# One subtraction of the last SwiGLU chunk on another engine, and two ScalarE functions in the other order

## The reference

```
norm(x, t; g, b) = (t Wg^T + g) * x / sqrt(mean(x^2) + 1e-6) + (t Wb^T + b)
y   = x + attention(norm1(x, cond))            # 16 heads of 16 channels, softmax over 64 keys
z   = y + (silu(n Wgate^T) * (n Whid^T)) Wout^T   with n = norm2(y, cond), 1024 hidden channels
out = x + z
```

## Time and profile before

| | |
|---|---|
| time, median of 3 runs | 1078.95 us (1076.1 to 1081.28) |
| profiled execution | 1077.67 us, span 1075.9 us, mean TensorE clock 0.992 |
| TensorE busy | 1032.2 us, 96% |
| VectorE busy | 673.7 us, 63% |
| ScalarE busy | 423.5 us, 39% |
| GpSimd busy | 339.5 us, 32% |
| DMA | 21.67 MB, 20 GB/s over the span |

### The profile page before, as it was taken

One profiled execution on the slowest core, in us unless ns is written; L12 is line 12 of the kernel. 1 busy time (PEld: TensorE's weight loads), 2 busy tenths in 40 slices (PEclk: granted clock), 3 DMA queues, 4 the chain that ended last, 5 costly groups with the idle time before them and its releaser, 6 DMA issues.

```text
span 1075.9 us, 22083 instructions
## 1 busy us (share of the span) xinstructions
PE 1032.2 (96%) x8240; PEld 919.7 (85%) x8240; DVE 673.7 (63%) x1306; ACT 423.5 (39%) x903; POOL 339.5 (32%) x284
## 2 busy tenths in 40 slices
PE   6879999999999999999999999999999999999987
PEld 5768889889888988988888888988988898898876
DVE  4645766566666656766666676657666665666543
ACT  3433343444334343343434434344433434334232
POOL 4313233232333223233232323323233323324142
PEclk9979999999999999999999999999999999999999
DMA  4100000010100001010010100001010000100000
GB/s 169 41 1 21 2 24 18 1 39 0 39 0 19 19 0 39 0 39 0 0 39 0 39 0 25 14 0 39 0 39 0 19 19 0 39 0 21 1 21 19
DMA packets 18968, 21.67 MB, mean 20 GB/s; under 512 B 640, under 2 KB 18240, under 8 KB 18816
## 3 DMA queue, kind: packets, MB, share of 16 engines
q1 hardware_dynamic: 18720, 21.24, 5.9%
q10 hardware_dynamic: 224, 0.10, 0.0%
HBM read 12.95 MB, written 8.39 MB: 20 GB/s over the span
## 4 chain that ended last, share of the span: by engine, by line
PE 67%; issue 23%; POOL 5%; ACT 2%; DVE 2%; DMA 0%; POOLq 0%; ACTq 0%; DVEq 0%; SPq 0%
PE ps L824 8%; PE ps L737 6%; PE ps L809 6%; PE ps L739 6%; PE ps L738 5%; PE ps L817 5%; PE ps L832 4%; PE ps L842 4%; PE ps L845 4%; PE ps L835 4%; PE ps L843 4%; PE ps L833 4%; POOL h_lo L247 4%; PE ps L744 1%; PE ps L853 1%
## 5 line engine op out<-in xcount | busy, mean ns | idle before, releaser
L247 POOL TENSOR_TENSOR h_lo<-shared,h_hi 128x512 fp32r<-128x512 f32 x128 | 164.7, 1286 | 360.5 <-ACT h_hi L371 313.3
L577 DVE SCALAR_TENSOR_TENSOR shared<-shared,ps 128x512 f32<-128x512 f32 x128 | 87.8, 686 | 128.1 <-ACT shared L366 127.6
L737 PE MATMUL ps<-out_w_hi,h_hi 128*128 128x256 f32 x512 | 154.1, 301 | 9.5 <-POOL h_lo L247 9.5
L366 ACT ACTIVATE shared<-ps 128x512 f32<-128x512 f32 x128 | 76.4, 597 | 194.1 <-PE ps L835 125.2
L739 PE MATMUL ps<-out_w_hi,h_lo 128*128 128x256 f32 x512 | 144.4, 282 | 0.0
L738 PE MATMUL ps<-out_w_lo,h_hi 128*128 128x256 f32 x512 | 143.7, 281 | 0.0
L824 PEld LDWEIGHTS ps<-values,probsT 128*128 128x128 f32 x1024 | 129.8, 192 | 13.2 <-ACT probsT L376 8.0
L376 ACT ACTIVATE probsT<-ps 128x512 f32<-128x512 f32 x128 | 74.7, 597 | 163.8 <-PE ps L817 163.8
L824 PE MATMUL ps<-values,probsT 128*128 128x66 f32 x1024 | 130.8, 271 | 4.0 <-ACT probsT L376 4.0
L371 ACT CAST h_hi<-shared 128x512 fp32r<-128x512 f32 x128 | 78.9, 616 | 99.7 <-DVE shared L584 99.7
L563 DVE TENSOR_REDUCE row_max<-ps 128x8 f32<-128x512 f32 x128 | 87.8, 686 | 37.7 <-PE ps L809 36.7
(11 more groups left out here) (101 smaller groups left out, 2150.9 us busy)
## 6 DMA issues: line engine op xcount, KB each, us to landing
x_in<-in_x SPq DMA_DIRECT2D x16, 512.0 KB, 3.4
out<-result SPq DMA_DIRECT2D x15, 512.0 KB, 2.9
shared<-in_attT SPq DMA_DIRECT2D x1, 1024.0 KB, 7.0
shared<-in_gateT SPq DMA_DIRECT2D x1, 1024.0 KB, 8.9
shared<-in_hidT SPq DMA_DIRECT2D x1, 1024.0 KB, 4.8
shared<-in_outT SPq DMA_DIRECT2D x1, 1024.0 KB, 5.5
out<-result SPq DMA_DIRECT2D x2, 256.0 KB, 2.2
result<-in_modT SPq DMA_DIRECT2D x1, 256.0 KB, 4.7
```

Source lines behind the costliest of these rows:

```text
L247: nc.gpsimd.tensor_tensor(h_lo[:, j % 2, :], h[:, :], h_hi[:, j % 2, :].bitcast(F32), ALU.subtract).then_inc(h_lo_done, 1)
L737: nc.tensor.matmul(dst, a_hi, b_hi, start=first, stop=False, skip_group_check=skip)
```

## The change

The low half of chunk 7 (the last of a tile) is formed by VectorE between its h of that chunk and the gains of the second normalisation, in place of GpSimd. It waits for the cast of chunk 7, for the low half of chunk 6 (still from GpSimd, so that the shared counter stays in order), and for the down product that used the same buffer. In ScalarE's list the exponential of pair 0 stands ahead of the tanh of chunk 0.

```diff
@@ GpSimd, iteration
                     inverse_rms(t, ms2, ms2_done, mse2, mse2_done, inv2, inv2_done, scaled2)
-                if mlp:
-                    low_hidden(t - 1, 7)
                 if attend:
                     low_norm2(t, 0)
@@ ScalarE, iteration
                 if alone(t):
                     keep_input(t)
+                if attend:
+                    exp(t, 0)
                 if mlp:
                     tanh(t - 1, 0)
                 if attend:
-                    exp(t, 0)
                     exp(t, 1)
@@ VectorE
+            def last_low_hidden(u):
+                j = CHUNKS - 1
+                dve.wait_ge(h_hi_done, CHUNKS * u + j + 1)
+                dve.wait_ge(h_lo_done, CHUNKS * u + j)
+                wait(dve, down_mm, CHUNKS * u + j - 1)
+                nc.vector.tensor_tensor(h_lo[:, j % 2, :], h[:, :], h_hi[:, j % 2, :].bitcast(F32),
+                                        ALU.subtract).then_inc(h_lo_done, 1)
@@ VectorE, iteration
                 if mlp:
                     act_and_gate(t - 1, 7)
+                    last_low_hidden(t - 1)
                 if attend:
                     for c in range(CH):
                         gain(t, c, 2, PAIR + 2 + c, xT2_done, xn2, xn2_lo_done, gained2)
```

## The result

The changed kernel takes 1072.90 us (median of 18 runs, 1066.94 to 1074.84), the kernel before 1079.53 (18 runs, 1076.06 to 1081.46): a ratio of 0.9931, 95% interval 0.9917 to 0.9946. The profiled execution took 1071.17 us, span 1069.4.

A forecast was written before the change was run, and what follows sets the result against it. TensorE's work (busy 96% of the span) plus its standstills bounds the kernel. Seams 8.0 + last tile 0.57 - seam behind iteration 15 0.44 - exchange 0.6 = 7.5 us less, so 1070.8 us, range 1067.5 to 1075.

The forecast's parts named there:

- down product earlier, 14 seams: Tile seams behind iterations 1 to 14: TensorE's last down product starts 0.57 us earlier each, 8.0 us in all.
- gains later: VectorE's gains and shifts of the next normalisation, queued behind the new subtraction, start 0.08 to 0.23 us late.
- scores and low passes wait: TensorE behind the seam: neither score products nor first chunk's low passes wait; 0.7 us of cover left at the latter.
- tanh late by the exchange: ScalarE behind the seam: tanh of chunk 0 starts 0.04 us late, costing 0.6 us over 15 iterations.
- new wait of the gate product: TensorE's gate product of chunk 1 would wait 0.3 to 0.5 us for h of chunk 0, 15 times.
- distance of the iterations: Time from one tile seam to the next falls from 63.83 to 63.30 us; forecast wrong if unchanged or below 63.1.
- seam behind iteration 15: Seam without scores or attention, low passes already waiting for GpSimd's xn_lo: later gains cost 0.44 us (0.3 to 0.55).
- end of the last tile: Nothing covers the subtraction there, so moving it to VectorE saves 0.57 us (0.5 to 0.63).
- The forecast's base: Starting time for the 7.5 us gain, set between the profiled 1077.67 us and the three-run median 1.3 higher.
- Rival A: Gate product of chunk 1 held only by TensorE's queue, so the exchange gains 4 us or more: 1066 or lower; chance 0.05.
- Rival B: TensorE's seam gain spent waiting at scores or low passes, half of 8 us or more gone: 1074 to 1078; chance 0.10.
- Rival C: Late exp 0 holds tanh, h of chunk 0 and gate product; slower from 0.54 us delay, 1078.6 or 1090; chance 0.05.

The follow-up runs named there:

- e1: Changed kernel without its exchange (tanh of chunk 0 again ahead of exp 0), only the low half of chunk 7 on VectorE: 1072.31 us, ratio to before 0.9928.
- e2: Kernel before with only the exchange (exp 0 ahead of tanh 0), low half of chunk 7 still on GpSimd: 1082.62 us, ratio to before 1.0028.
- e7: Changed kernel with the chunk 7 subtraction made twice on VectorE, the first into a spare buffer: 1083.16 us (one run).
- e3: Changed kernel with the probabilities-times-values product of pair 1 moved ahead of the gate product of chunk 1 on TensorE: 1068.65 us, ratio to before 0.9903.
- e5: e3 plus down product of chunk 0 ahead of pair 2's transposes and cast of chunk 1 ahead of exp 2: 1064.67 us, ratio to before 0.9871.
- e8: Changed kernel with GpSimd's first weight subtraction waiting until VectorE has scaled the first tile's rows: 1068.77 us, ratio to before 0.9912.

## Why the prediction was right, step by step

| step | predicted | measured |
|---|---|---|
| subtraction starts behind the cast | 0.03 to 0.13 | 0.04 (523.62 to 523.66) |
| its length, and to the down product | 0.69, 0.05 | 0.69, 0.05 |
| down product earlier, 14 seams | 0.57 (0.53 to 0.63) | 0.63 |
| gains later | 0.08 to 0.23 | 0.04 |
| scores and low passes wait | no | no; cover 0.8 us |
| tanh late by the exchange | 0.04 (0 to 0.1) | 0.11 |
| new wait of the gate product | 0.3 to 0.5, 15 times | 0.48, 15 times |
| distance of the iterations | 63.30 | 63.37 |
| seam behind iteration 15 | 0.44 slower | 0.40 slower |
| end of the last tile | 0.57 faster | 0.61 faster (cast to down product 1.39 to 0.78) |
| time | 1070.8 (7.5 us less on its base) | 1072.90 (6.6 us less) |

The mechanism was right in both parts, and e1, e2 and e7 show it by themselves. Two sizes were off. The low half was taken at 0.57 and gave 0.63, the upper bound: the third wait cost nothing (0.04 behind the cast, as with one). The exchange was taken at 0.04 and cost 0.11, just outside its bounds: I let exp 0 start 0.03 behind its transposes, as other pairs do, but it starts 0.11 behind the end that the profile models for them (529.95 + 0.60 = 530.55 to 530.66), and tanh, 0.49 behind exp, comes 0.14 behind the complete gate bank instead of 0.03. The later transposes of the same seam (531.31 + 0.60, exp 531.94) show 0.03. Why pair 0 is later stays open; the modelled end of transposes that are followed at once by wide products may be the place. Another 0.03 to 0.04 us per iteration, between the gate product and the next transposes (53.56 to 53.60 in this seam, 53.56 to 53.59 in the mean of 13 iterations), has no cause that I can show; each part alone has 0.02 to 0.03 there too.

With these sizes the sum is 14 x 0.63 + 0.61 - 0.40 - 15 x 0.11 - 14 x 0.04 = 6.8 us, against 6.6 between the medians and 6.5 between the profiled spans. The forecast's base was the weaker point: I set 1070.8 between one profiled run and a median of three, and that median (1078.95) was 0.6 below the one of 18 runs. Of the 2.1 us between forecast and time, 1.2 are the base (1078.3 against 1079.53) and 0.9 the gain.

Rival A failed as worked out: h of chunk 0 held the gate product. Rival B was true in one seam of fifteen. Rival C named the right place, but the delay there was 0.11, not the 0.54 it needed, and each of the eleven profiles has one load of a function table, 1.28 us at the start, none between exp and tanh. In e2, with no gain beside it, the exchange lengthened every iteration. The spacing of exp and tanh was 0.49 us (530.66 to 531.15), by the row; the estimate of 0.52 worked out from the Trainium skill ("ScalarE: Activation LUTs", section "What ACT_TABLE_LOAD costs") is not what this kernel shows, and where the two differ the row stands.

## What to carry to other kernels

When two waits end at the same moment, removing the earlier one gives nothing: look at what the next instruction waits for, and ask whether the removal delays that. The stall is then moved, not gone, and it shows under a new name (here 0.27 us before one product became 0.48 before the next). In this kernel it paid only with ready work put into it (0.31 and 0.30 us per iteration in e3 and e5, together more than the 0.47 of the change). Take a repeating kernel's distance between iterations as the measure: it settled 0.1 us where whole runs scattered by 8. Then look at what it leaves out: over the eleven profiles the transposes behind iteration 1 came between 141.79 and 147.49 us, and the clock in iteration 15 moved e1 by 1.3.

## What the runs showed of the hardware that I had not expected

The four scalings of the first tile on VectorE (SBUF to SBUF) took one of three lengths over eleven profiles: 1.14, 3.23 or 5.3 us, 2.1 apart. It went with the time at which GpSimd's two subtractions of 128 x 1024 elements, 2.35 to 2.5 us each there, start beside them: 0.13 to 0.32 us behind the first scaling gave 5.3, 0.65 to 0.74 gave 3.23, 0.96 (e2) or later gave 1.14, as if both, one or none of them stood in front of the last scaling. GpSimd's start hangs on a cast that waits for the DMA of the weights (0.13 to 0.96 us behind the first scaling in the nine profiles where nothing orders the two). A single scaling takes 0.34 us, the longest in the changed kernel 2.44, and with GpSimd held back in e8 all four are short again. The Trainium skill, "SBUF — State Buffer", section "SBUF: two separate sides", says that VectorE, in its two-port modes or with two inputs in SBUF, shares a pair of ports with GpSimd, which whoever starts first holds for its whole instruction. The rows agree: in the changed kernel the scalings end at 9.68 + 3.23 = 12.91, 0.15 behind the end of GpSimd's first subtraction (10.40 + 2.36). That the scalings ran in such a mode is not shown by a row. Inside the iterations the same pair meets at 551.76 (GpSimd 1.27) and 551.93 (scalings, 2.04 instead of 1.14), where TensorE does not wait for it.

```profile
551.76 1.27 POOL L247 TENSOR_TENSOR h_lo<-shared,h_hi 128x512 fp32r<-128x512 f32 x1
551.93 2.04 DVE L497 TENSOR_SCALAR x_scaled<-x_in,inv 128x256 f32<-128x256 f32 x4 [2.93 <-POOL inv L229]
```

The new VectorE subtraction reads two SBUF operands and, by the same section, could have met the same; GpSimd was idle around it for 5.96 us, and it took 0.69.
